# A fused attention and FFN kernel: an order of steps for each engine, and PE steps that can be taken in two halves

## The reference, cut to what matters

```python
x = x + _L0_attn_ref(_layernorm(x), ...)   # linear attention, 16 heads: phi(q) (phi(k)^T v), phi = silu + 1
x = x + _L0_ffn_ref(_layernorm(x), ...)    # silu(x w1) * (x w2), then gelu(h h1), gelu(h h2), then w3
x = x + _L1_attn_ref(_layernorm(x), ...)   # softmax attention over the tile's 512 tokens, one head
x = x + _L1_ffn_ref(_layernorm(x), ...)    # tanh of one folded 256 x 256 product, plus bias
...
h = silu(_tlin(x, w1_w, w1_s)) * _tlin(x, w2_w, w2_s)     # 256 -> 1024
h = gelu(_tlin(h, h1_w, h1_s)); h = gelu(_tlin(h, h2_w, h2_s))   # 1024 -> 1024, twice
return _tlin(h, w3_w, w3_s)                                # 1024 -> 256
```

## Time and profile before

| | |
|---|---|
| median of 3 runs (range) | 2118.21 us (2117.63 to 2120.3) |
| the profiled execution, its own time | 2119.35 us |
| its span, first to last instruction | 2117.6 us |
| busy share PE, PEld, DVE, ACT, POOL | 95%, 91%, 56%, 40%, 18% |
| mean granted clock of TensorE | 0.991 of full speed |
| DMA engines, mean over the span | 95% busy in the first fortieth, 5% in the second, 0 tenths after that |

### The profile page before, as it was taken

How to read it: one execution, slowest core, us unless ns; L and a number is a source line. 1 busy time by engine, 2 the same in 40 slices (tenths; PEclk the granted TensorE clock), 3 DMA queues, 4 the chain that set the end, 5 groups by cost and what they waited for, 6 DMA issues and landing times.

```text
span 2117.6 us, 37472 instructions
## 1 busy us (share of the span) xinstructions
PE 2008.2 (95%) x15484; PEld 1926.5 (91%) x15484; DVE 1189.6 (56%) x2881; ACT 836.7 (40%) x1538; POOL 373.9 (18%) x347
## 2 busy tenths in 40 slices
PE   6899999999999999999999999999999999999985
PEld 5798999989999998999989999998999989999985
DVE  4555656456565555656456565555656456565544
ACT  2334434344333444434344333444434344333422
POOL 1111211112121011211112121011211112121011
PEclk9999999999999999999999999999999999999997
DMA  9500000000000000000000000000000000000000
GB/s 361 184 3 2 21 1 1 21 1 21 1 21 1 1 21 1 21 1 1 21 1 21 1 21 2 1 21 1 21 1 1 21 1 11 1 11 1 1 11 10
DMA packets 24421, 46.01 MB, mean 22 GB/s; under 512 B 1152, under 2 KB 21376, under 8 KB 24064
## 3 DMA queue, kind: packets, MB, share of 16 engines
q1 hardware_dynamic: 24240, 43.41, 5.8%
HBM read 35.02 MB, written 19.92 MB: 26 GB/s over the span
## 4 chain that ended last, share of the span: by engine, by line
PE 79%; DVE 8%; ACT 5%; DMA 3%; issue 2%; POOL 1%; SPq 0%; DVEq 0%; ACTq 0%; POOLq 0%
PE ffn_fill L857 41%; PE att_fill L818 21%; PE ffn_fill L818 8%; PE ffn_fill L915 6%; PE att_fill L873 2%; DVE whole L585 2%; ACT L786 2%; DMA scratch_h2T<-in_h2T 1%; ACT whole L756 1%; PE att_fill L991 1%; ACT kv_b L786 1%; DVE st L520 1%; DMA scratch_h1T<-in_h1T 1%; POOL act_lo L503 1%; DVE sm L661 1%
## 5 line engine op out<-in xcount | busy, mean ns | idle before, releaser
L857 PE MATMUL ffn_fill<-act_hi,h 128*128 128x256 f32 x4096 | 989.7, 284 | 8.8 <-DVE flag L722 3.3
L857 PE MATMUL ffn_fill<-act_lo,h 128*128 128x256 f32 x4096 | 980.6, 281 | 0.0
L857 PEld LDWEIGHTS ffn_fill<-act_hi,h 128*128 128x128 f32 x4096 | 773.5, 189 | 16.2 <-POOL act_lo L503 6.3
L857 PEld LDWEIGHTS ffn_fill<-act_lo,h 128*128 128x128 f32 x4096 | 774.6, 189 | 3.7
L594 DVE CAST act_hi<-whole 128x512 fp32r<-128x512 f32 x256 | 109.2, 426 | 618.6 <-ACT whole L756 618.6
L756 ACT ACTIVATE whole<-ffn_fill,scales 128x256 f32<-128x256 f32 x512 | 215.1, 471 | 493.0 <-PE ffn_fill L857 491.9
L818 PE MATMUL ffn_fill<-half_hi,w 128*128 128x256 f32 x1024 | 251.4, 287 | 12.8 <-DVE whole L585 9.4
L818 PE MATMUL ffn_fill<-half_lo,w 128*128 128x256 f32 x1024 | 247.2, 282 | 0.0
L503 POOL TENSOR_TENSOR act_lo<-whole,act_hi 128x512 fp32r<-128x512 f32 x128 | 166.8, 1303 | 368.2 <-DVE act_hi L590 367.6
L490 POOL TENSOR_TENSOR rstd_B<-var_eps_B,minus_half 128x2 f32<-128x2 f32 x32 | 22.6, 707 | 1176.7 <-DVE var_eps_B L527 1176.7
L818 PEld LDWEIGHTS ffn_fill<-half_hi,w 128*128 128x128 f32 x1024 | 194.7, 190 | 15.8 <-issue 15.8
(11 more groups left out here) (156 smaller groups left out, 3161.6 us busy)
## 6 DMA issues: line engine op xcount, KB each, us to landing
x<-in_L_attn_x SPq DMA_DIRECT2D x16, 512.0 KB, 3.5
out<-x SPq DMA_DIRECT2D x16, 512.0 KB, 3.0
h<-scratch_h1T SPq DMA_DIRECT2D x1, 4096.0 KB, 18.2
h<-scratch_h2T SPq DMA_DIRECT2D x1, 4096.0 KB, 14.4
w<-scratch_w1T SPq DMA_DIRECT2D x1, 1024.0 KB, 16.0
w<-scratch_w2T SPq DMA_DIRECT2D x1, 1024.0 KB, 19.3
w<-scratch_w3T SPq DMA_DIRECT2D x1, 1024.0 KB, 6.4
rows<-in_rows SPq DMA_DIRECT2D x1, 640.0 KB, 5.7
```

The lines of the kernel that those rows point to most:

```text
L857: last = pe.matmul(two(bank)[:, o, :], view(w), view(moving[:, k, :]), start=k == 0 and o == 0 and half == 0, stop=k == KH - 1 and half == ...
```

## The change

Each engine now has a table with an order of its own for FIRST, BODY and LAST; prologue and TAIL keep the plan. The numbering of banks and the semaphore values still come from PLAN: `steps_of` first walks the plan and keeps a copy of the counts for every step, then runs the steps in the engine's order with the counts kept for them. On PE a step can be named with a or b: its first and its second half (a half of G, H or W is 16 matmuls, of U one of its two banks). No instruction is removed or added but for branches that go with the split steps in FIRST and in a variant that this input does not take.

```diff
+def order_from(plan):
+    return [(steps_from(word.rstrip("ab"))[0], word[len(word.rstrip("ab")):]) for word in plan.split()]
+PE_ORDERS = {
...
+    "BODY": order_from("""
+    U0 U1 U2 U3 G0 G1a c:T G1b G2a c:CV c:CZ G2b c:CS0 G3 c:CP0 c:CS1 c:CS2 c:CO0 H0a c:CP1 c:CS3 H0b c:CO1
...
-        def steps_of(part, steps, counts, slots):
+        def steps_of(part, steps, counts, slots, order):
+            at = {}
             for step in steps:
-                part(step, counts, slots)
+                at.setdefault(step, []).append(counts.copy())
                 counts.ahead(step)
+            for step, piece in order or [(step, "") for step in steps]:
+                here = at[step][0] if piece == "a" else at[step].pop(0)
...
+            def halves(piece, n):
+                return range(n // 2 if piece == "b" else 0, n // 2 if piece == "a" else n)
...
                 def emit(view):
-                    for k in range(KH):
+                    for k in halves(piece, KH):
                         if j == 0 and k % 2 == 0:
                             pe.wait_ge(s["ffn_ready"], c.value("ffn_ready", k // 2 + 1 - PAIRS))
...
-                    last.then_inc(done, 1)
+                    if piece != "a":
+                        last.then_inc(done, 1)
...
-                    a_bank, a_done = to_fill(pe, c, "ffn_fill", 0)
-                    b_bank, b_done = to_fill(pe, c, "ffn_fill", 1)
-
                     def emit(view):
-                        for which, (bank, done) in enumerate(((a_bank, a_done), (b_bank, b_done))):
+                        for which in halves(piece, 2):
+                            bank, done = to_fill(pe, c, "ffn_fill", which)
```

More of the change, by code:

```diff
@@ L188, in ahead, with copy @@
             self.now[name] = self.now.get(name, 0) + n
+    def copy(self):
+        other = Counts(self.now, self.rate, self.it)
+        other.seen = dict(self.seen)
+        return other
 STAGE_OF = {"AST": "A", "BST": "B", "CST": "C", "DST": "C"}
@@ L207 @@
 TAIL = only("c")
+def order_from(plan):
+    return [(steps_from(word.rstrip("ab"))[0], word[len(word.rstrip("ab")):]) for word in plan.split()]
+PE_ORDERS = {
+    "FIRST": order_from("""
+    U0 U1 U2 U3 CHECK1 G0 G1 G2 G3 CHECK2 H0 H1a CHECK3 H1b H2 H3 BT1 W0a a:T W0b U0 U1 a:AKV0 U2 U3a a:AKV1
+    a:AKV2 a:AKV3 U3b G0a a:AS a:AQ a:AM G0b G1 a:AOa G2a a:AOb G2b G3 H0 H1 H2 H3 n:BT0 W1"""),
+    "BODY": order_from("""
+    U0 U1 U2 U3 G0 G1a c:T G1b G2a c:CV c:CZ G2b c:CS0 G3 c:CP0 c:CS1 c:CS2 c:CO0 H0a c:CP1 c:CS3 H0b c:CO1
+    c:CP2 H1a c:CO2 H1b c:CP3 H2 c:CO3 H3 BT1 W0 U0a c:T U0b U1 c:CF U2a a:T U2b U3 G0a a:AKV0 a:AKV1 a:AKV2
+    a:AKV3 G0b G1 G2 a:AS a:AQ a:AM G3 a:AO H0 H1 H2 H3 n:BT0 W1"""),
+    "LAST": order_from("""
+    U0 U1 U2 U3 G0 G1 c:T G2 c:CV c:CZ G3a c:CS0 G3b H0 c:CP0 c:CS1 c:CS2 H1a c:CO0 c:CP1 c:CS3 H1b c:CO1
+    c:CP2 H2a c:CO2 c:CP3 H2b H3 BT1 W0 U0 U1 U2 U3 c:CO3 G0 G1 G2 G3 H0 H1 c:T H2 H3 W1 c:CF"""),
+}
@@ new lines @@
+DVE_ORDERS = {
+    "FIRST": order_from("""
+    U0 U1 LOOK12 LOOK13 U2 CHECK1 U3 G0 G1 LOOK20 LOOK21 LOOK22 LOOK23 CHECK2 G2 G3 LOOK30 H0 CHECK3 BST1 H1
+    BNO1 a:AST H2 a:ANO H3 BT1 W0 a:T U0 U1 U2 a:AKV0 a:AKV1 a:AKV2 a:AKV3 U3 a:AS a:AQ a:AM G0 a:AO G1
+    n:BST0 n:BNO0 G2 G3 H0 H1 H2 H3 n:BT0 W1"""),
+    "BODY": order_from("""
+    U0 U1 U2 U3 c:CST c:CNO c:T G0 c:CQ c:CV c:CZ G1 c:CS0 c:CP0 c:CS1 G2 c:CS2 G3 c:CO0 c:CP1 c:CS3 c:CO1
+    c:CP2 H0 c:CO2 BST1 c:CP3 H1 BNO1 a:AST c:CO3 c:DST H2 H3 BT1 c:DNO W0 c:T U0 a:ANO c:CF U1 a:T U2 U3
+    a:AKV0 G0 a:AKV1 a:AKV2 a:AKV3 a:AS G1 G2 a:AQ a:AM a:AO G3 n:BST0 n:BNO0 H0 H1 H2 H3 n:BT0 W1"""),
+    "LAST": order_from("""
+    U0 U1 U2 U3 c:CST c:CNO G0 c:T G1 c:CQ G2 c:CV c:CZ c:CS0 G3 c:CP0 c:CS1 c:CS2 c:CO0 H0 c:CP1 c:CS3
+    c:CO1 c:CP2 c:CO2 BST1 H1 c:CP3 BNO1 H2 H3 BT1 W0 U0 U1 U2 U3 c:CO3 G0 c:DST G1 c:DNO G2 G3 c:T H0 H1 H2
+    H3 W1 c:CF"""),
+}
@@ L210, in build @@
+POOL_ORDERS = {
+    "FIRST": order_from("""
+    U0 U1 U2 U3 BST1 a:AST U0 U1 U2 a:AB U3 n:BST0"""),
+    "BODY": order_from("""
+    U0 U1 U2 U3 c:CST c:CB BST1 a:AST c:DST U0 c:CF U1 U2 a:AB U3 n:BST0"""),
+    "LAST": order_from("""
+    U0 U1 U2 U3 c:CST c:CB BST1 U0 U1 U2 U3 c:DST c:CF"""),
+}
 def build(nc, a):
@@ L510, in part @@
                     last.then_inc(s["out_ready"], 1)
-            walk(part)
+            walk(part, POOL_ORDERS)
         @block.vector
@@ L1041, in _ @@
             pe.wait_ge(consts, 7)
-            walk_first(part)
+            walk_first(part, PE_ORDERS)
             pe.wait_ge(all_checked, 1)
```

87 lines of the change are left out of this document (54 added, 33 removed).

## The result

The changed kernel takes 2042.65 us (median of 4 runs, 2041.96 to 2043.49) against 2119.05 us before (4 runs, 2117.63 to 2120.3): a ratio of 0.964, with a 95% interval of 0.9623 to 0.9657, or 76.4 us less. I had forecast 2055 us with a range of 2046 to 2082.

What follows compares the result with a forecast made beforehand. PE was taken as the bound, only its idle time winnable: BODY 58.7, LAST 3.65, CF 1.0 and FIRST 1.3 make 64.7 us; 2119.35 less 64.7 and 1.1 gives 2053.5, leaned to 2055, range 2046 to 2082.

Steps and rivals of the forecast that it cites:

- The seven places: PE stalls in a BODY iteration, 4.52 us together; all but G0's 0.33 were to go.
- the thin margins: Places such as CP0 (0.15 us to spare) and the `a:` T, cleared only just; forecast moved from 2053.5 to 2055.
- CP1's gain: BODY, before CP1: H0a's 1.9 us of matmuls cover the wait for CS1's exponential; gain 1.48 us.
- 4.19 per iteration: BODY: sum of the six stalls to be removed, in us; 14 times makes 58.7 us.
- The 0.33 stays: BODY, G0's 25th matmul: its wait on the chain from U3's last matmul stays at 0.33 us.
- 3.65: LAST: its first pass repeats the first five gains of BODY, 3.65 us.
- CF behind W1 1.0: LAST: CF moved into PE's idle time behind W1 gains 1.0 us, bounded by 0 and 2.8.
- about 1.3 us can go, between 0 and 3: FIRST: PE's waiting before CHECK2 shrinks by about 1.3 us, between 0 and 3.
- New waits: Rival, chance 0.20: new waits from late results take half the gain back, 2069 to 2090 us.
- A price for cutting: Rival, chance 0.03: leaving and resuming unfinished accumulations costs PE; slower from 0.6 us per cut, 2153 at 1 us.
- Order doesn't matter: Rival, chance 0.03: stalls come from chains no order shortens and reappear one step later; about 2115 to 2120 us.
- more (0.04): Rival, chance 0.04: the G0 stall shrinks too and FIRST gives its 3 us; 2040 to 2048 us.

Runs made afterwards that it cites:

- h0_back: The changed kernel with H0 taken whole behind CP1 again by PE in BODY, as in the kernel before: 2055.9 us.
- cst_back: The changed kernel with the statistics CST back behind U0 on DVE and POOL in BODY: 2056.72 us.
- g0_cut: The changed kernel with G0 also cut on PE in BODY and LAST, G1a between its halves: 2038.95 us.
- only_first: The changed kernel with the engines' own orders kept for FIRST alone, BODY and LAST in the plan's order: 2114.79 us.
- more_cuts: The changed kernel with the H steps of BODY's second pass taken in interleaved halves, four more steps cut: 2044.05 us.
- whole_a: The changed kernel with no step cut on PE, each split step taken whole at the place of its first piece: 2164.68 us.
- whole_b: The changed kernel with no step cut on PE, each split step taken whole at the place of its second piece: 2131.2 us.
- ano_back: The changed kernel with DVE in BODY taking norm ANO behind the second T's copies and U0, U1 ahead of CF, as before: 2050.57 us.
- only_last: The changed kernel with the engines' own orders kept for LAST alone, FIRST and BODY in the plan's order: 2111.81 us.

## Why the prediction came out 12 us short

**What bounds it.** Right: PE's idle time was nearly all that there was to win. The prediction said that the iteration would take 122.9; it takes 122.33.

**The seven places.** Right in place and sign. U3, CV, CP0, CO0, CP1 and the `a:` T lost their whole wait, and the thin margins that I had leaned towards, 1.5 us, all held: at CP0 there were 0.37 us to spare, not 0.15. Two reasons were incomplete, as h0_back and cst_back show: the order of ACT and DVE had a share of 0.58 in CP1's gain, and the stall before U3 had its continuation in G0.

**The size of the BODY term: the step that failed.** "4.19 per iteration" against 4.72, 14 times 0.53, 7.4 us; by the first pair of profiles BODY gained 65.9 instead of 58.7. With this alone set right the forecast would be 2047.8, inside the range; FIRST, below, adds 4.2 and puts it at 2043.6, outside. I took from each stall only the distance to the matmul that waits. But the row behind a stall is slower too, in the trace of the kernel before as well. PE's timeline there, behind the stall before U3 and behind the one in G0:

```profile
809.14 0.28 PE L818 MATMUL ffn_fill<-half_lo,w 128*128 128x256 f32 x1
...
814.30 0.28 PE L857 MATMUL ffn_fill<-act_lo,h 128*128 128x256 f32 x1
```

By the starts in the earlier trace rows, 809.14 - 808.94 = 0.20 and 814.30 - 814.08 = 0.22 instead of 0.12. Over the iteration this makes some 0.36 more at the six places that were cleared (0.07 to 0.08 each at U3, CV and CO0, 0.03 to 0.06 at the transposes of CP0, CP1 and T). g0_cut tried it on the seventh: with the stall gone, the row behind it was back at 0.12. The remaining 0.14 is G0: "The 0.33 stays" was wrong, it is 0.18 now. Its chain got shorter by as much. POOL's timeline, U3's low part in the kernel before and then in the changed one:

```profile
812.64 1.38 POOL L503 TENSOR_TENSOR act_lo<-whole,act_hi 128x512 fp32r<-128x512 f32 x1 [0.36 <-DVE act_hi L590]
```

```profile
782.54 1.30 POOL L568 TENSOR_TENSOR act_lo<-whole,act_hi 128x512 fp32r<-128x512 f32 x1 [0.60 <-DVE act_hi L655]
```

It ends 2.98 us behind the last matmul's slot of U3 (783.84 - 780.86) instead of 3.11 (814.02 - 810.91). In the kernel before, DVE's norm ran beside it; now the norm waits for POOL's power, which starts at 784.47, and comes later. No run was made for this alone, but the rows agree: a low part on POOL beside a norm takes 1.38 here, 1.38 in cst_back (789.39, with the norm at 789.23) and 1.40 in the changed kernel (840.37, beside ANO), and 1.29 or 1.30 without one. That is 0.08; another 0.06 is DVE's cast in front of it, 0.49 us at 812.07 beside the low part of U2, and 0.43 at 782.03, where POOL stands idle. The last 0.03 of the 0.53 I did not trace.

**LAST.** "3.65" was 4.8: the same slower rows, the part of G0, and 0.7 for a stall in the second pass's G0 (0.59 and the row behind it) which I had not counted and which `c:CO3`, now between U3 and G0, covers. "CF behind W1 1.0" was right: from W1's last matmul to TAIL's first T it is 7.16 us now instead of 5.49, with the 2.84 of CF in it, a gain of 1.17. The gap that is left:

```profile
1981.28 0.27 PE L883 MATMUL att_fill<-wf_hi,xt_lo 128*128 128x256 f32 x1
1985.64 1.31 PE L950 MATMUL att_fill<-ident,xn 128*128 128x128 f32 x8 [4.08 <-DVE xn L598]
```

It is 4.1 where I had said 4.5.

**FIRST: the second term that was too small.** "about 1.3 us can go, between 0 and 3" was 5.5 in the first pair of profiles. Over all profiles whose PE orders are those of the kernel before or of the change (3 and 9), from the trace:

| | order before | changed order |
|---|---|---|
| FIRST | 117.2 to 119.6, mean 118.3 | 113.1 to 116.9, mean 114.9 |
| from the first LOOK of h2 to H0's first matmul | 10.0 to 11.0, mean 10.3 | 7.2 to 9.5, mean 7.9 |
| landing: from FIRST's first matmul to the first LOOK of h2 | 26.2 to 29.3, mean 27.8 | 26.3 to 29.2, mean 27.8 |
| first pass of H0 to H3 on PE | 16.7 to 16.9, mean 16.8 | 15.35 in six, 15.8 to 16.9 in three |

So the order is worth about 3.4: 2.4 from the checks, within my bounds but near the upper end, and 1.1 from the clock, for which I had no term. With three profiles on one side this is a rough figure; only_first's time, 2.5 with 1.3 to 5.3, allows it. Behind H3, where PE has a new order in FIRST too, both take 63.4 to 63.5 on average. The clock in the first profiles, FIRST of the kernel before, then of the changed one, each for 5.4 us from H0's start:

```profile
86.96:92.40 5.44, 5.43 (x33) 5.44 (x34) 0.60 (x1) 0.00 (x0) 0.00 (x0) 0.69 0.39 115
```

```profile
82.92:88.40 5.48, 5.48 (x46) 5.48 (x47) 3.21 (x5) 1.78 (x4) 0.00 (x0) 1.00 0.40 129
```

Before, PE stood still for 1.70 and 1.49 us around CHECK2 and then had a granted clock of 0.69 over this stretch, with 33 matmuls done; now the waits are shorter and 46 are done. The 5.5 of the first pair are 2.3 from the checks, 1.5 from the pass of H0 to H3 and 1.5 from the landing. The landing differs by up to 3 us from profile to profile with either order and has the same mean, so its share was luck. Why the clock falls in some profiles and not in others with nearly the same gaps was not tried.

**The sum.** By the first pair of profiles: BODY 65.9 (58.7 forecast), LAST 4.8 (3.65), CF 1.2 (1.0), FIRST 5.5 (1.3), and the start and the end together 0.0: 77.4, as the spans have it; 64.7 was forecast. The missing 12.7 and the 1.5 that I had leaned towards thin margins make 14.2; against them stand the 1.1 that I had taken off for the profiled execution of before, and the 0.7 by which that of the changed kernel lay below its median. That leaves the 12.4 between 2055 and 2042.65.

**The rivals.** New waits: none on PE in the iteration. A price for cutting: nothing, by more_cuts. Order doesn't matter: it does, most of the idle time is gone. With PE's order as it is, the orders of the other engines pay for 0.58 at CP1 (h0_back) and for the 0.94 that cst_back loses; at the `a:` T they pay only together with U2a. The case "more (0.04)" came true for both of its reasons, a smaller stall in G0 and more from FIRST, and for the slower rows, which it did not name. Part of FIRST's share was the luck of the landing. Still, its chance was too small: all my terms for stalls were lower bounds of what a stall costs, and the margins were the only thing that I had weighed on the other side.

## What to carry to other kernels

Where one engine bounds and its idle time is a few short waits, put independent work ahead of each wait, in pieces as long as the wait, and give each other engine the order in which its results are wanted; an accumulation could be left and taken up again here at no cost. The two belong together: the same orders with whole steps were slower than the plan, so a new order is to be walked on every engine with its cover. Price a stall by two rows, the one that waits and the one behind it, and look at the granted clock behind any gap of some microseconds; sum the whole pass, since a delay that has no wait at one place shows up at the next.

## What the runs showed of the hardware

- A matmul of 256 columns takes 0.12 us start to start, also when its predecessor belongs to another unfinished bank: in more_cuts four more cut steps per iteration left it at 122.33 us. The row behind a stall takes 0.20 to 0.22, even behind one of 0.2 us (CV).
- A long distance right behind a very short one is no stall. AM's last matmul starts 0.03 before the first of G3, and that takes 0.30, in every kernel here; together that is the 0.21 of an AM matmul and 0.12. Behind a row of transposes it is 0.03 and 0.20, for 0.11 and 0.12.
- After 2.9 us with 0.28 us of matmuls the granted clock was 0.50 for 3.2 us (whole_a); after the waits of 0.9 to 1.6 us of whole_b it stayed at 1.00 over the whole iteration.
- Much the same gap can go either way. Between FIRST and BODY the starts of two matmuls lie 2.2 to 2.7 us apart in all 14 profiles; in five of them (ano_back, cst_back, more_cuts, only_last, whole_a) the granted clock was 0.61 to 0.70 over the next 3 us, in nine it was 1.00. In three of the five (ano_back, cst_back, more_cuts) the first iteration took 1.4 to 1.6 us more than the later ones, which is as much as some effects looked for here; compare iterations and stretches, not only times.
